# A graph network on one core: the column-tiled sums of two edge groups placed back to back on PE

## What is computed

```python
h  = relu(LN(x))                                   # 1250 x 512
agg = seg((h[src] + edge_attr) @ Wm.T + bm) / max(deg, 1)
x1 = x + LN(h + gelu([h, agg] @ Wu.T + bu)) * gamma + beta
h1 = relu(LN(x1))
out = x1 + relu(((1 + eps) * h1 + seg(h1[src])) @ W1 + b1) @ W2 + b2 + h1
```

## Time and profile before

| | us |
|---|---|
| median of 3 runs | 491.05 (490.82 to 491.95) |
| the profiled execution's own time | 492.31 |
| its span, first to last instruction | 490.5 |
| PE busy in the span | 473.2 |
| DVE busy | 269.6 |
| ACT busy | 158.1 |
| POOL busy | 122.2 |
| first sums, first piece, last sums start at | 24.9, 190.0, 248.1 |

### The profile page before, as it was taken

The page is one execution under the profiler, slowest core; times in us unless marked ns, Lnnn a source line. Parts: engine busy times, 40 slices in busy tenths (PEclk is TensorE's granted clock), DMA queues, the critical chain, the costliest instruction groups (busy, mean ns, idle before and its releaser), DMA issues.

```text
span 490.5 us, 9290 instructions
## 1 busy us (share of the span) xinstructions
PE 473.2 (96%) x3275; PEld 277.9 (57%) x3275; DVE 269.6 (55%) x621; ACT 158.1 (32%) x291; POOL 122.2 (25%) x183
## 2 busy tenths in 40 slices
PE   4999999999999999999999999799999999999997
PEld 3445555555455446776765656699844449544442
DVE  4789878787878888877857789923100000011011
ACT  6726633332333338411037377630012122000000
POOL 4005433444343432000001112339990000000000
PEclk9999999999999999989999999999999999999999
DMA  8998999999999999988430102040140000010111
GB/s 293 383 353 294 404 386 391 390 409 403 396 385 391 403 408 409 384 328 272 169 109 23 43 23 60 0 172 1 20 152 1 0 0 1 21 43 21 44 43 38
DMA packets 31640, 98.92 MB, mean 202 GB/s; under 512 B 3592, under 2 KB 4616, under 8 KB 31594
## 3 DMA queue, kind: packets, MB, share of 16 engines
q1 hardware_dynamic: 30458, 97.27, 52.7%
q10 hardware_dynamic: 1136, 1.05, 0.7%
HBM read 95.76 MB, written 2.56 MB: 200 GB/s over the span
## 4 chain that ended last, share of the span: by engine, by line
PE 81%; DVE 10%; DMA 4%; issue 2%; SPq 1%; POOL 1%; DVEq 0%; POOLq 0%
PE ps L1354 14%; PE ps L1339 14%; PE ps L1090 10%; PE ps L1136 7%; PE ps L1189 6%; PE ps L1109 6%; PE ps L1190 5%; PE ps L1286 4%; PE ps L1098 4%; DMA X<-in_x_dram 4%; PE ps L1118 4%; PE ps L1262 3%; PE ps L1263 3%; DVE A L695 2%; DVE stats L776 1%
## 5 line engine op out<-in xcount | busy, mean ns | idle before, releaser
L421 POOL TENSOR_TENSOR aggT<-turned_sums,aggT 128x88 f32 x118 | 62.5, 529 | 88.1 <-ACT turned_sums L486 74.9
L1024 DVE TENSOR_TENSOR U<-ps,U 128x512 f32<-128x512 f32 (+1 forms) x10 | 6.9, 692 | 128.4 <-PE ps L1354 128.4
L695 DVE TENSOR_TENSOR A<-ps,A 128x220 f32 x158 | 60.7, 384 | 28.6 <-PE ps L1109 18.0
L1354 PE MATMUL ps<-W2s,hid 128*128 128x512 f32 (+1 forms) x160 | 68.8, 592 | 0.0
L1339 PE MATMUL ps<-aggT,W1s 128*128 (+1 forms) x192 | 67.3, 513 | 0.0
L1090 PE MATMUL ps<-ea,oneD 128*22 128x256 f32 x944 | 62.7, 383 | 0.0
L1339 PEld LDWEIGHTS ps<-aggT,W1s 128*128 128x128 f32 x192 | 36.4, 190 | 30.7 <-issue 30.6
L1354 PEld LDWEIGHTS ps<-W2s,hid 128*128 128x128 f32 (+1 forms) x160 | 30.0, 188 | 38.2 <-issue 38.2
L480 ACT COPY packed_sums<-ps 128x256 f32<-128x256 f32 x59 | 22.0, 372 | 91.5 <-PE ps L1090 91.5
L1090 PEld LDWEIGHTS ps<-ea,oneD 128*22 128x22 f32 x944 | 22.6, 101 | 46.5 <-issue 21.7
L1262 PE MATMUL ps<-AR,Hh 128*128 128x256 f32 (+1 forms) x160 | 44.1, 311 | 1.0 <-DVE Hl L991 1.0
(11 more groups left out here) (133 smaller groups left out, 641.7 us busy)
## 6 DMA issues: line engine op xcount, KB each, us to landing
ea<-in_edge_attr_dram SPq DMA_DIRECT2D x78, 1024.0 KB, 7.9
X<-in_x_dram SPq DMA_DIRECT2D x1, 2304.0 KB
xt<-in_x_dram SPq DMA_DIRECT2D x9, 256.0 KB, 2.8
out_dram<-U SPq DMA_DIRECT2D x9, 256.0 KB
W1s<-in_L_gnn_W_dram SPq DMA_DIRECT2D x1, 2048.0 KB, 8.8
W2s<-in_L_gnn_W_dram SPq DMA_DIRECT2D x1, 2048.0 KB, 8.4
WuN<-in_L_gnn_Wu_dram ACTq DMA_DIRECT2D x2, 512.0 KB, 4.2
WuN<-in_L_gnn_Wu_dram SPq DMA_DIRECT2D x1, 1024.0 KB, 7.0
```

The costliest lines, as they stand in the source:

```text
L421: nc.gpsimd.tensor_tensor(cols, sums, cols, ALU.add).then_inc(early_step, 1)
L695: V.tensor_tensor(cols, ps[:, 4 + m % 2, half * KW:(half + 1) * KW].rearrange("p (h w) -> p h w", w=W), cols, ALU.add).then_inc(add_step, 1)
L1354: last = T.matmul(ps[0:rows, 6 + b % 2, :], hid[:, k, b * P:b * P + rows], W2s[:, k, :], start=k == 0, stop=k == KC - 1)
```

## The change

The list PAIRED groups the loop steps in twos: [0], [1, 2], ... [57, 58], then [59], then [60, 61] to [76, 77], and [78]. For a pair, PE's queue now holds the sums of both groups directly one behind the other, then both turns, the degree products if they fall in it, then the counts of both steps, one of them ahead of each step's other work and what is left behind both, then both pieces. Only PE's order changes. The semaphores and what each instruction waits for, the orders of DVE, ACT, POOL and SP, the buffers and the amount of work stay as they are.

```diff
     EARLY = FULL + 1
+    PAIRED = [[0]] + [[n, n + 1] for n in range(1, FULL, 2)] + [[n for n in (k, k + 1) if n < NG] for k in range(FULL + 2, NG, 2)]
+    PAIRED.insert(1 + FULL // 2, [FULL + 1])
+    assert sum(PAIRED, []) == list(range(NG)) and FULL % 2 == 0 and [GEN_AT - 1, GEN_AT] in PAIRED
...
-            for n in range(NG):
-                sums(n)
-                if 0 < n <= EARLY:
-                    turn(n - 1)
-                if n == DEG_AT - 1:
-                    degree_products()
-                for m in COUNTS[n]:
-                    counts(m)
+            def besides(n):
                 for b in range(NT):
                     for f in range(1, FC):
                         if U_AT[b][f] == n:
                             u1(b, f)
                 if n in ASIDE:
                     aside(*ASIDE[n])
-                if n == GEN_AT:
+
+            for pair in PAIRED:
+                for n in pair:
+                    sums(n)
+                for n in pair:
+                    if 0 < n <= EARLY:
+                        turn(n - 1)
+                if DEG_AT - 1 in pair:
+                    degree_products()
+                counting = [m for n in pair for m in COUNTS[n]]
+                for n in pair:
+                    for m in counting[:1]:
+                        counts(m)
+                    counting = counting[1:]
+                    besides(n)
+                for m in counting:
+                    counts(m)
+                if GEN_AT in pair:
...
-                if n >= PIECE_AT:
-                    piece(n - PIECE_AT)
+                for n in pair:
+                    if n >= PIECE_AT:
+                        piece(n - PIECE_AT)
```

## The result

The changed kernel takes 498.28 us in the median of 4 runs (497.33 to 499.44), the kernel before 490.94 (490.50 to 491.95) beside it: ratio 1.0133, with a 95% interval of 1.0110 to 1.0156, or 6.5 us slower. The forecast was 491.7, in a range of 488.0 to 494.5. The profiled execution took 498.16 us (span 496.4), 5.9 more than that of before. The first group's sums start at 25.71 instead of 24.89 us, but this is no loss of its own. In other runs that start moves between 24.9 and 26.8 and group 7 does not follow it: in the order of before, with DVE's work left whole, group 7's sums start at 48.8 to 49.2 us in four traces (group 0 from 24.9 to 26.8), in the changed order at 50.1 to 50.5 in seven (group 0 from 25.7 to 26.8).

A forecast was written before the change was run, and what follows sets the result against it. PE, busy 96%, was taken as the bound, DVE and DMA within some per cent; group 61's +1.87 and late pairs' -2.3 made -0.45, the clock +1.1: +0.65 us on the 491.05 median, 491.7, range 488.0 to 494.5.

The forecast's parts named there:

- What is saved: On PE, 0.29 us for each pair, 29 early and 9 late: 11.0 us if nothing else were late.
- Rival 5: At the pairs' sums, no drain is saved: 11 us gone, half absorbed by waits, 497 us; chance 0.05.
- Waits on DVE in a cycle: Counting part, six groups: 0.75 of 0.87 us saved is lost to waits, so 15.9 us instead of 16.1.
- B's third count and C's second sums: Second and third pairs of six groups, three counts each: PE waits 0.5 us for adds, then 0.25 for oneD.
- Rival 2: Counting part: the DVE waits don't come as walked, group 57 some 2.5 us earlier, 488.5 to 489.5; chance 0.16.
- rival 3: Counting part: DVE's lag does not clear within a cycle, 8 x 0.6 = +4.8 us, 496; chance 0.15.
- The start: Up to group 9: DVE stays the bound, sums 2 directly follow sums 1, 0 to 0.3 us gained.
- The loads: DMA: group 6's load 5.5 us earlier fills the hole, 2.5 us ahead; group 60's 1.1 us wait goes.
- the -0.7: Sum of the counting part's terms to the start of group 57: 0.7 us earlier, bounds -2.5 and +1.
- The clock: At group 61, PE's stand of 3.3 us lets the clock fall, dense pieces pay +1.1 us.
- Rival 1: The clock stays up at group 61: 490.6 us; chance 0.20.
- rival 4: The clock falls in the counting part too, 1.1 us each time; two falls make it slower; chance 0.06.

The follow-up runs named there:

- the column with five buffers: The changed kernel with a fifth load buffer for groups 0 to 54 instead of four: 496.06 us, ratio 1.0085.
- The filled stand: The changed kernel with three full-width matmuls of unused result between the sums of groups 60 and 61: 496.35 us, ratio 1.0093.
- both repaired: The changed kernel with a fifth load buffer and groups 60 and 61 one by one: 493.40 us, ratio 1.0033.
- the run with late pairs only: The kernel before with only groups 62 to 77 paired, groups up to 61 one by one: 490.53 us, ratio 0.9972.

## Why the prediction was wrong

Forecast +0.65 us by the profiled execution, measured +5.9. The step that failed is the pricing of the counting part up to group 61, forecast 0.0 to +0.1 us and measured +5.2, by loads that come late, by the start of the loop and by DVE. By the steps of the prediction:

- **What is saved: right.** Sums 0.88 to 0.89 apart (0.87 forecast); 0.28 a pair where nothing is late, 0.31 to 0.35 late, for 0.29. Rival 5, no drain saved, is refuted. The Trainium skill, TensorEngine Tiling (Array Packing), section Tiling Modes, says that a change of the tiling mode drains TensorE; the 0.28 us a pair agree with it.
- **Waits on DVE in a cycle: right in place, slightly too small.** They stand before B's third count and C's second sums. In the steady stretches 13 to 25 and 37 to 43 six groups gained 0.07 to 0.09 us, not 0.2 (16.03 us, 15.9 forecast, 16.11 before). Shortening DVE's one-hots took 5.9 us off the changed kernel and 1 off the one before. Rival 2 is refuted, and so is rival 3: the lag clears, each cycle repeats the one before.
- **The start: wrong in sign.** "0 to 0.3 us gained there" and "Turns and ACT's copies [...]: each needs the group before only [...]; nothing" were the steps. At 41.5 us PE stood 1.16 us for ACT's copy of group 3's sums, and the counts that had stood ahead of that wait now stood behind it. Group 7 came 1.3 us late (1.1 to 1.6 by the other traces of the changed order) instead of 0.2 early. A mean of 32% busy said nothing of ACT at that moment. That this wait is the whole cause is argued from the timeline; no run took the start by itself. All that isn't loads came to +3.1 up to group 61 (the column with five buffers), with 0.1 forecast.
- **The loads: the step that failed most.** "The load of group 6 goes out 5.5 us earlier, which fills the DMA hole: 2.5 us ahead from then on." The load of 6 did land 2.5 us earlier and that of 8 by 3.1. But the loads of 9 and 10 go out when the sums of 5 and 6 are done, and these were no earlier than before, so a new hole opened at 46 to 52 us; the load of 9 landed 0.95 us earlier, that of 10 at the same time. The prediction had taken a lead in one load for a lead in the stream. It then priced the loads at nothing for all pairs, although the second of a pair wants its load 0.9 us behind the first, where it had 2.6 us before, and two buffers are let go 0.9 us apart and then none for some 4 us. Measured: 2.1 us at group 61 by the buffer, 2.4 to 3.3 us of the whole. None of the five rivals had late loads as a cost (rival 2 had them as the end of a gain), although the prediction had read that all three partners are within some per cent of each other; this is why the range ended at 494.5.
- **Group 61: right.** 10.48 us after group 57 (10.35 forecast), 3.2 us of standing, released through `oneD` behind `turn_blocks`, and piece 0 late. Only "at 192.0 us as before" fell, with the -0.7 that should have stood ahead of it.
- **The clock: right, and larger.** It fell (PEclk 0.72 from 197 to 201 us), for 1.5 us instead of 1.1. The filled stand shows the cause. The Trainium skill, TensorE: Matmul & The Clock Gate, section Loop structure matters more than you think, says that a long wait between matmuls lets the clock drop; the run agrees. Rival 1 is refuted; so is rival 4, with PEclk 1.00 in all of 60 to 170 us.
- **Late pairs: right, a little small**, -2.8 for -2.3.

Shares of the 6.5 us: the pair [60, 61] 3.0, the loads 2.4. With both repaired 1.6 stay, and the trace of that kernel has the same 1.6: group 7 is 1.4 us late, 1.7 more come up to group 61, and the late pairs, the first with its wait, give 1.5 back. Which part of the 1.7 the cycles, the branch and the bank waits carry is read from the table alone; no run took them apart.

## What to carry to other kernels

Where two loads or two results are taken directly behind one another, their partners see bursts, though the mean stays as it is: count for each buffer ring when a place comes free in the new order, for many rounds, not for the first load that gets ahead. If three resources are within some per cent of each other, each needs its own rival, and pairing should start with the groups that ask the second resource for the least. Avoid a stand of some 3 us on TensorE ahead of dense matmuls, or fill it: here filling it kept the clock up.

## What the runs showed of the hardware

- The clock's fall at the degree products is not certain. In the kernel before it is granted at 0.50 from 217 to 220 us; in the run with late pairs only, PEclk was 1.00 from 214 to 220 us with the same 20 one-column matmuls, and from group 68's sums to group 70's it took 8.08 us instead of 9.58 in the changed kernel. 1.5 us of a profiled execution can hang on that, with no difference in the order.
- Within the two pieces behind group 61 the distance of the 512-column matmuls goes from 0.43 us (199.22 to 199.65) to 0.24 (202.67 to 202.91): the clock rose from its lower level of 1.2 GHz to 2.4 under the pieces themselves.
- Half the bytes, or one buffer of 1 MB more at full bytes, cured the same late loads. How two loads issued 0.9 us apart share the 16 DMA engines was not tried.
